# Expert products by pairs of hidden chunks, their fifth product as two half-height products on two strips of the array

## What is computed

```python
def _L0_ffn_ref(x, gate_w, gate_b, w1, b1, w2, b2):        # 32 experts
    gates = jax.nn.softmax(x @ gate_w + gate_b, axis=-1)
    h = jax.nn.gelu(jnp.einsum('btc,ech->bteh', x, w1) + b1, approximate=False)
    y = jnp.einsum('bteh,ehc->btec', h, w2) + b2
    out = jnp.einsum('bte,btec->btc', gates, y)
    return out
# layer 2, in _L2_ffn_ref: one MLP, then 4 experts mixed by top-2 gates
x = x + jax.nn.gelu(x @ mlp_w1 + mlp_b1, approximate=False) @ mlp_w2 + mlp_b2
he = jax.nn.gelu(xm @ exp_w1[e] + exp_b1[e], approximate=False)
oe = he @ exp_w2[e] + exp_b2[e]
# layer 3, in _L3_ffn_ref: one MLP
ffn = jax.nn.gelu(n2 @ W1 + bf1, approximate=False) @ W2 + bf2
```

## Time and profile before

| | |
|---|---|
| Median of 3 runs (lowest, highest) | 2928.49 us (2925.44 to 2933.19) |
| The profiled execution's own time | 2927.57 us |
| Its span, first to last instruction | 2925.8 us |
| Mean granted TensorE clock | 0.946 of full |
| TensorE busy (matmul) | 2689.8 us, 92% of the span |
| VectorE, ScalarE, GpSimd busy | 2051.2, 1052.6, 645.3 us |

### The profile page before, as it was taken

How to read it: one execution, slowest core, us unless ns; L and a number is a source line. 1 busy time by engine, 2 the same in 40 slices (tenths; PEclk the granted TensorE clock), 3 DMA queues, 4 the chain that set the end, 5 groups by cost and what they waited for, 6 DMA issues and landing times. The chain is left out here.

```text
span 2925.8 us, 61848 instructions
## 1 busy us (share of the span) xinstructions
PE 2689.8 (92%) x22697; PEld 2451.3 (84%) x22697; DVE 2051.2 (70%) x5175; ACT 1052.6 (36%) x2052; POOL 645.3 (22%) x816
## 2 busy tenths in 40 slices
PE   8889999999999999999999788799797889967778
PEld 7679999999999999999999677767466789956557
DVE  3867777776777777777777788723567676778877
ACT  2533333332333333323323444411355443324533
POOL 1312212122122122121221211021223201113561
PEclk9989999999999999999999899979898889978788
DMA  3101011011010010110100000057100100000000
GB/s 144 38 22 39 20 38 38 19 38 38 19 38 23 34 38 19 38 38 19 38 19 32 9 2 2 7 173 229 36 2 2 58 20 20 1 27 3 25 20 18
DMA packets 24481, 105.91 MB, mean 36 GB/s; under 512 B 4455, under 2 KB 9463, under 8 KB 19086
## 3 DMA queue, kind: packets, MB, share of 16 engines
q1 hardware_dynamic: 22654, 99.62, 9.9%
q0 software_dynamic: 1584, 3.30, 0.3%
HBM read 98.32 MB, written 6.64 MB: 36 GB/s over the span
## 5 line engine op out<-in xcount | busy, mean ns | idle before, releaser
L919 ACT ACTIVATE hid<-psum,dat 128x384 f32<-128x384 f32 (+1 forms) x912 | 554.2, 608 | 1144.1 <-PE psum L603 1029.9
L884 PE MATMUL psum<-w,hid_hi 128*128 128x384 f32 x2964 | 858.9, 361 | 2.2 <-DVE y_tok L935 1.6
L886 PE MATMUL psum<-w,hid_lo 128*128 128x192 f32 x2964 | 745.9, 252 | 0.0
L886 PEld LDWEIGHTS psum<-w,hid_lo 128*128 128x128 f32 x2964 | 571.0, 193 | 1.7
L884 PEld LDWEIGHTS psum<-w,hid_hi 128*128 128x128 f32 x2964 | 561.5, 189 | 5.5 <-issue 3.9
L953 DVE TENSOR_TENSOR hid_lo<-hid,hid_hi 128x384 fp32r<-128x384 f32 (+1 forms) x912 | 539.8, 592 | 31.5
L950 DVE CAST hid_hi<-hid 128x384 fp32r<-128x384 f32 (+1 forms) x912 | 340.7, 374 | 122.1 <-ACT hid L919 120.8
L976 DVE SCALAR_TENSOR_TENSOR h_tok<-psum,gate,h_tok 128x192 f32<-128x192 f32 x416 | 173.2, 416 | 248.0 <-PE psum L886 244.5
L603 PE MATMUL psum<-xa_hi,w_hi 128*128 128x384 f32 (+1 forms) x912 | 324.2, 356 | 1.6 <-ACT hid L919 0.5
L603 PE MATMUL psum<-xa_lo,w_hi 128*128 128x384 f32 (+1 forms) x912 | 322.4, 353 | 0.0
L603 PE MATMUL psum<-xb,w_lo 128*128 128x384 f32 (+1 forms) x912 | 321.8, 353 | 0.0
(11 more groups left out here) (367 smaller groups left out, 4213.8 us busy)
## 6 DMA issues: line engine op xcount, KB each, us to landing
raw<-in_L_exp SPq DMA_DIRECT2D x36, 1344.0 KB, 5.7
w_e<-in_L_exp SPq DMA_DIRECT2D x20, 576.0 KB, 4.0
w_e<-in_L_exp SPq DMA_DIRECT2D x20, 384.0 KB
pix<-in_pixels SPq DMA_DIRECT2D x6, 832.0 KB, 10.3
w_e<-in_L_exp SPq DMA_DIRECT2D x20, 195.0 KB
raw<-in_L_mlp SPq DMA_DIRECT2D x2, 1344.0 KB, 5.8
wp_raw<-in_L_att SPq DMA_DIRECT2D x1, 2304.0 KB, 8.3
route_rows<-in_rows_clear SPq DMA_DIRECT2D x1, 2000.0 KB, 22.9
```

The costliest lines, as they stand in the source:

```text
L884: nc.tensor.matmul(o[:, 0:2 * D], hid_hi[k % 2][:, m, c], w2[j][:, m, :], start=m == 0, stop=False)
L886: ins = nc.tensor.matmul(o[:, 0:D], hid_lo[k % 2][:, m, c], w2[j][:, m, 0:D], start=False, stop=m == HC - 1)
L919: nc.scalar.activation(hid[(6 * k + m) % 3][:, 0:128 * nt], bank[4 + (6 * k + m) % 4][:, 0:128 * nt], func, bias=bias).then_inc(s["h_act"] ...
```

## The change

The loop of `up` goes by two chunks. For each of the pair it issues the first four products of all 128 rows into its own bank; then come the two fifth products, back to back, each of 64 rows only: the first takes partitions 0 to 63 of `w1_lo[.., 1, ..]` and `xb`, the second partitions 64 to 127 of `w1_lo` and of a new tile `xb_twin`, which holds there another copy of what `xb` has on partitions 0 to 63. Each of the two signals `h_full`. `xb_twin` is written by ScalarE, one more activation (64 partitions) after each `high(i)` ahead of an expert phase, which waits for `high(i)` itself to have landed; a new counter `twin_full` tells TensorE of it. Left out of the sum with this is the low part of the weights times the low part of features 128 to 191, which the fifth product had included.

```diff
+        xb_twin = sb("xb_twin", [128, XP], F32R)
...
-        def x_made(eng, at, cols):
+        def x_made(eng, at, cols, twin_at=None):
 
             group = [128 * (t0 + n) >= cols for t0, n in TBLK].index(True)
             eng.wait_ge(s["lo_full"].sem, at + group + 1)
+            if twin_at is not None:
+                eng.wait_ge(s["twin_full"].sem, twin_at + group + 1)
...
                     ins.then_inc(s["hi_full"].sem, 1)
+                    if ahead_of == "experts":
+
+                        c = slice(128 * t0, 128 * (t0 + n))
+                        act.wait_ge(s["hi_full"].sem, b["hi_full"] + i + 1)
+                        ins = nc.scalar.activation(xb_twin[64:128, c], xb[0:64, c].bitcast(F32), ACT.Identity)
+                        ins.then_inc(s["twin_full"].sem, 1)
...
-                    for m in range(HC):
-                        n = 24 * e + 6 * k + m
-
-                        if is_first(e):
-                            x_made(pe, x_at, 1280 if k == 0 and m > 1 else 128 * (t0 + nt))
-                        pe.wait_ge(s["h_act"].sem, b["h_act"] + n - 3)
-                        o = bank[4 + (6 * k + m) % 4][:, 0:128 * nt]
-                        mc = slice(128 * m, 128 * m + 128)
-                        five(o, [w1_hi[j][:, 0, mc], w1_hi[j][:, 1, mc]],
-                             [w1_lo[j][:, 0, mc], w1_lo[j][:, 1, mc]],
-                             xa_hi[:, c], xa_lo[:, c], xb[:, c], True).then_inc(s["h_full"].sem, 1)
+                    for m in range(0, HC, 2):
+                        o = [bank[4 + (6 * k + m + y) % 4][:, 0:128 * nt] for y in range(2)]
+                        for y in range(2):
+                            n = 24 * e + 6 * k + m + y
+
+                            if is_first(e):
+                                x_made(pe, x_at, 1280 if k == 0 and m + y > 1 else 128 * (t0 + nt), twin_at)
+                            pe.wait_ge(s["h_act"].sem, b["h_act"] + n - 3)
+                            mc = slice(128 * (m + y), 128 * (m + y) + 128)
+                            for z, (w, x) in enumerate(((w1_hi[j][:, 0, mc], xa_hi), (w1_hi[j][:, 0, mc], xa_lo),
+                                                        (w1_lo[j][:, 0, mc], xa_hi), (w1_hi[j][:, 1, mc], xb))):
+                                nc.tensor.matmul(o[y], w, x[:, c], start=z == 0, stop=False)
+                        for y, x in enumerate((xb, xb_twin)):
+
+                            half = slice(64 * y, 64 * y + 64)
+                            nc.tensor.matmul(o[y], w1_lo[j][half, 1, 128 * (m + y):128 * (m + y) + 128], x[half, c],
+                                             start=False, stop=True).then_inc(s["h_full"].sem, 1)
```

More of the change, by code:

```diff
@@ L224, in vit_tower @@
                  "px_full", "av_full", "av_used", "t_full", "t_used", "out_done", "bridge", "k_done",
-                 "o_split", "it_dve", "holds", "root", "normed", "hi_full", "scale_full", "lo_full", "hi_step", "rel_table", "att_hi", "att_ready"]
+                 "o_split", "it_dve", "holds", "root", "normed", "hi_full", "scale_full", "lo_full", "hi_step", "rel_table", "att_hi", "att_ready", "twin_full"]
         s = {n: signal(n) for n in names}
@@ L426, in features_phase @@
             b = base(t_full=4, t_used=1 + len(on_dve), dve_step=1 if keep is not None else 0,
-                     root=2 if keep is not None else 1, normed=len(on_act), hi_full=4, scale_full=1, lo_full=4,
+                     root=2 if keep is not None else 1, normed=len(on_act), twin_full=4 if ahead_of == "experts" else 0, hi_full=4, scale_full=1, lo_full=4,
                      hi_step=4 if ln else 0)
@@ L594, in features_phase @@
             x_from["lo_full"] = b["lo_full"]
+            x_from["twin_full"] = b["twin_full"]
             return dict(first=inner)
@@ L794, in experts_phase @@
             STEPS = 24 + TILES
-            x_at = x_from["lo_full"]
+            x_at, twin_at = x_from["lo_full"], x_from["twin_full"]
             def is_first(e):
```

## The result

The changed kernel takes 3030.39 us (median of 4 runs, 3021.63 to 3034.01) against 2927.97 (2925.44 to 2933.19, 4 runs) for the kernel before: a ratio of 1.0344, 95% interval 1.0328 to 1.0360. That is +102 us; the forecast was +97 and 3025 us.

A forecast was written before the change was run, and what follows sets the result against it. TensorE's stream in `up` was taken as the bound. The terms -172.6 removed, +86.3 halves, +182.4 height changes and +1 twin gave +97 us on 2927.6, so 3025 us, 3.3% slower, range 2995 to 3080 (8 in 10).

The forecast's parts named there:

- Removed, 172.6: In `up`, two full-height fifth products go from each of 456 pairs: 172.6 us less.
- the halves, +86.3: In `up`, two 64-row products a pair run fully side by side, 0.175 or 0.232 us a pair: 86.3 us added.
- rival B: In `up`, the halves don't overlap, in their loads (3074 us) or wholly (3111 us); chance 0.12.
- Height, +182.4 at 0.40 us a pair: In `up`, changing product height there and back costs draining and a bare load each way: 182.4 us over 456 pairs.
- C: At height changes in `up`, only the drain is paid, the load being pulled ahead: 2927 us, no change; chance 0.08.
- D: In `up`, heights change freely: 2842 us; decided by a there and back under 0.19 us; chance 0.06.
- Rival E: TensorE's granted clock falls in a tenth of `up`, as streams fill less of it: +64 us, 3089 us; chance 0.08.
- Late signals, costed at nothing: A pair signals `h_full` at its end, so the even unit reaches ScalarE about 1 us later; costed at nothing.
- the cover that the prediction named: In `up`, bank reuse two pairs later; ScalarE 0.6, VectorE 0.87 us a unit, 1.75 a pair against TensorE's 1.97.
- The twin, +1 (0 to 5): Four extra ScalarE activations ahead of each of four expert phases, delaying the first Gelu: +1 us in all, 0 to 5.

The follow-up runs named there:

- one_strip: Changed kernel with both 64-row fifth products of a pair on the first strip (partitions 0 to 63); 3107.04 us, one run.
- lone_halves: Kernel before, one unit at a time, each fifth product cut to 64 rows on the first strip, twin and its waits added; 3294.41 us.
- shared_hid4: Changed kernel, every second pair issuing its halves first (7 instead of 12 there-and-backs an expert), plus a fourth `hid` buffer; 2960.38 us, 1.0107 of kernel before.
- full_pairs: Changed kernel with its pairs, late signals and twin, but fifth products again of 128 rows; 2948.83 us, 1.0065 of kernel before.
- no_swap_hid4: Changed kernel with `up` as nine slots of two 64-row products a pair, half of each sum omitted, fourth `hid` buffer; 2923.37 us, 0.9986 of kernel before.

## Why the prediction came out right, by its steps

- **Removed, 172.6, and the halves, +86.3.** Right. Steps between full-height products are unchanged; the halves start in the same hundredth, and one strip instead of two costs 77 us against the 86.3 that rival B gave for no overlap, in one run. B is out in both its forms (3074 and 3111, against 3107.04 for one_strip, which is B's second form made real).
- **Height, +182.4 at 0.40 us a pair.** Right, and measured in three ways: 0.402 (lone_halves), 0.394 (shared_hid4 against the changed kernel, layer 0), and from the result itself (102 - 1 + 86.3) / 456 = 0.41. The timeline shows both parts where the prediction put them, 0.09 of draining and 0.107 of bare load each way; a pair of 384 takes the predicted 1.97 us. C fell with it: no load of one height is recorded under a stream of the other. So did D, whose point of decision was 0.19. The Trainium skill ("TensorEngine Tiling (Array Packing)", Key Properties, 1) says that changing the tiling mode drains TensorE; the trace agrees and gives the price, which counts the bare load too.
- **The clock.** 1.00 in 720 to 1650 us of layer 0, also with two changes of height in every pair of 2 us. Rival E is out there.
- **Late signals, costed at nothing.** Right for layer 0 of this kernel, and only because the cover that the prediction named holds: with a pair at 1.97 us TensorE doesn't wait on `h_act` in layer 0. The prediction said that without that cover the wait would be for `h_act`, and full_pairs, with a pair at 1.75, shows it: its layer 0 phase is 7.3 us longer than before. The prediction's figures for ScalarE and VectorE, 0.6 and 0.87 a unit, are paces within a run of units. They leave out that the pairs make VectorE start each run of units up to 0.9 us later; with three `hid` buffers and TensorE at 0.876 a unit it doesn't make that up before TensorE needs the bank. That is why one edit can cost nothing beside another and 7 us alone. The rest of the 21 us of full_pairs is in the short phases and partly the twin's.
- **The 5 us between +97 and +102.** The interval of the ratio goes from +96 to +105 us, so they need no cause. The table of phases has +84.3, +13.8 and +4.5 where the sum gives 80.8, 12.6 and 2.5; layer 3's +2.0 beyond its share was also seen with pairs alone (+2.4). I take it for the same effect, which isn't proved.
- **The twin, +1 (0 to 5).** Too small as a middle value, within its bounds, and the path was read too short. The first product of layer 0 starts at 179.6 us in the changed kernel and 174.5 before, but at 174.6 in one_strip, which has the same twin and waits; so the start varies from run to run and the twin isn't seen in it. Ahead of layer 2's MLP the first Gelu starts 3.9 us after the first product, where it was 2.1 before, and TensorE waits 0.58 us for it: the table load is pushed as forecast (0.6 to 1.3 us), by some more. What the prediction didn't see is the split of the weights behind the twin ahead of layer 2's experts, which makes their first product 2.0 us later, twice the whole term.

What stays open: some 5 us of the price of pairs and twin in layer 2's MLP and between the layers, the clock's part in layer 3, and whether a kernel that does the whole sum on two strips at one height, with features and weights mirrored on both halves of the array, would keep the 4 us of no_swap_hid4. That one has no run; copies of features and weights would come on top for other engines, of which VectorE already is the bound there.

## What to carry to other kernels

Rows that are saved in a matmul saved nothing by themselves here (one_strip's second half took a whole step); two short products on two strips do, but only if products of one height follow each other, since going there and back cost 0.40 us, more than two whole products of 384 columns (0.35). Count changes of height first, and gather the short products: from 12 to 7 changes an expert gave 63 us back in layer 0 (with the fourth `hid` buffer). And an activation that is put on an idle engine can still push what stands behind it in the queue, as the twin does ahead of layer 2's experts. And before TensorE is made faster, set the next engine's time a unit beside it, including when it gets its first work at each turn of the loop: here VectorE at 0.87 us stood right behind TensorE at 0.876, and took what no change of height would have given.

## What the runs showed of the hardware that was not expected

- Height can be changed twice in each pair of 2 us at a full granted clock (1.00 over 720 to 1650 us of the changed kernel), and matmul records then cover more of the time (930.00 of 930 us) than in the faster kernel (926.15 of 930): the busy share hides bare loads and draining.
- Runs of 64-row products on two strips keep the pace of full-height ones (no_swap_hid4: slots at 1002.02 and 1002.20, records of 0.34), so within a run two loads, one for each strip, are hidden in one slot of 0.175 us. The first slot after a wait shows its load bare (0.45).
- One buffer more of 128 x 512 was worth some 16 us in shared_hid4 and nothing measurable in the kernel before.
